# A graph network kernel: runs of edges grouped by destination block and by two source blocks instead of one

## The chip, the cores and the metric

The kernel runs on one core of one Trainium2 chip. The metric is device time in microseconds (us) of one execution. Three runs of the kernel before gave 11165.87, 11168.30 and 11169.82 us; the median is 11168.3.

## The reference

There are 6250 nodes of 32 channels and 106250 directed edges (50000 random pairs in both directions, and one loop per node). Four graph layers follow each other, each as x = x + layer(relu(layernorm(x))): a Gaussian mixture layer, a two-step neighbourhood mean with a hidden width of 64, a spline convolution (with a small network that moves each edge's position) and a two-step neighbourhood sum. Both layers with two steps have this core, used four times in all:

```
summed = segment_sum(x[src], dst, num_segments=N)     # gather rows by source, add them by destination
h = relu(summed/deg @ W_l + b + x @ W_r)
out = segment_sum(h[src] ..., dst) ...                # and again
```

All results are float32.

## The kernel before, in words

Nodes stand in 49 blocks of 128 (NB), node b*128+p in partition p. A "tile" is 128 edge slots, one per partition. Edges are kept in three orders: by source (880 tiles), by destination, and by spline cell. In destination order a tile holds edges of one destination block only.

**Runs.** Within a destination block the edges are also ordered by source block, and each group of one destination block and one source block is padded to a multiple of 8. Eight consecutive slots are a "run" (RUN = 8). `place_by_runs` (lines 686 to 797) works out these places from counts. The worst case of the padding sets the size of everything in destination order: TILES_D = 1008 tiles (line 43), which every loop goes over, filled or not.

**Sending.** `send_runs` (904 to 991) gathers the source rows. Runs are sorted by source block; 128 runs of one source block are a "set", and the table has SSETS = 176 sets (line 48). Per set VectorE compares the eight local numbers of each run with the lane (`hot`, line 940: a one-hot matrix of 128 x 1024), TensorE multiplies each of eight 128 x 128 parts of it with the 112 columns of that source block (line 955, eight slots, each a weight load and a matmul), ScalarE copies the 896 columns out of PSUM into `rec` (line 969), and GpSimd scatters 128 rows of 1792 bytes to `run_rows` in DRAM (line 986). The rings: `loc` (the local numbers, broadcast to all partitions, one 2 MB DMA by SyncE for 8 sets, line 927) has two halves of 8 sets, `hot` and PSUM have 4 places, `rec` has 16. ScalarE refills a half of `rec` when the scatters of that half have landed (line 966). Padding entries have an index beyond the table, so their rows are not written.

**Summing.** `sum_runs` (993 to 1163) reads `run_rows` back in batches of 8 tiles (126 batches) by a plain DMA and adds the rows by destination: per tile a weight load and a matmul of 66 columns and a weight load and a matmul of 33 columns (lines 1075, 1077). The two functions are called four times in turn. In the second call (with `planes`) the same batches also carry the network's outputs of both ends of the edge to GpSimd, which takes their difference.

**Other loops over TILES_D.** `destination_order_pass` (1930 to 2104, 42 turns of 6 batches of 4 tiles) forms the first layer's messages and scatters each tile to the cell order with GpSimd (line 2099). `to_cells` (2325 to 2380) does the like for the spline convolution (line 2375, 63 turns of 16 tiles). The sort by new cell (2554 to 2582) has TILES_D columns and 64 bins. `source_runs` (1177 to 1293) finds each run's place, over DSETS = 126 columns of runs in chunks of 24, and `job_send_ids` scatters their numbers (126 scatters) while the messages are summed. `rec_d` and `run_rows` are blanked by DMAs before use (line 494 and line 422).

The engines keep in step by semaphores written out by hand; stages are divided by barriers (`next_phase`), so a stage's end is that of its last engine.

## Time and profile before

| | |
|---|---|
| median of three runs | 11168.3 us |
| profiled execution | 11236.53 us, span 11234.7 us |
| busy: PE, DVE, ACT, POOL | 54%, 48%, 21%, 61% of the span |
| mean granted TensorE clock | 0.602 of full speed |
| mean DMA rate | 96 GB/s |

PE is TensorE's matmuls and PEld its weight loads, DVE is VectorE, ACT ScalarE, POOL GpSimd, SP SyncE. "L986" is line 986. A row of a group gives the line, engine, operation, what it writes and reads, and the number of times; then the busy time and the mean duration in ns; then the idle time of the engine just before those instructions and what ended it. The lines of the page show a kernel of many stages in which no engine is busy throughout; each stage has to be read by itself. In the granted clock 1.00 is 2.4 GHz and 0.50 is 1.2 GHz.

### The profile page before, as it was taken

To read this page: it belongs to the slowest core of one execution; us is meant where nothing else is said; L and a number is where in the kernel's file an instruction comes from. 1 tells how busy PE (TensorE), PEld (TensorE's weight loads), DVE (VectorE), ACT (ScalarE), POOL (GpSimd) and SP (SyncE) were. 2 spreads that over 40 slices of the span, in tenths; PEclk is the share of its full clock that TensorE was granted. 3 is DMA by queue.
4 is the path that set the end of the run, shared out by engine and by line. 5 is a ranking of instruction groups with operands and counts; after the bars stand their busy time and mean duration, and the time that the engine had idled before them with its cause. 6 is when DMAs were issued, how large, how long until landed. Compare 5 with 4: busy or idle time off the path is not lost. (4 is left out here: it accounts for less than half of the span.)

```text
span 11234.7 us, 164281 instructions
## 1 busy us (share of the span) xinstructions
PE 6072.8 (54%) x41365; PEld 4946.0 (44%) x41366; DVE 5445.1 (48%) x9318; ACT 2323.2 (21%) x6227; POOL 6797.1 (61%) x7082
## 2 busy tenths in 40 slices
PE   5200056665677775666555556655555555554555
PEld 1200035554566674444443445434444444443444
DVE  9300075555555556888783535641111333374535
ACT  0000024443233331111104141011111111124040
POOL 0677727777577776777434146447777777765151
PEclk9555577777555557788656555565555555556565
DMA  9960012221333331111375556762000111126565
GB/s 367 207 63 5 5 44 83 82 83 66 94 100 102 99 100 41 53 53 53 77 157 217 140 208 172 158 54 26 13 13 9 25 28 28 27 51 253 110 248 113
DMA packets 1380904, 1074.85 MB, mean 96 GB/s; under 512 B 949835, under 2 KB 1216095, under 8 KB 1369239
## 3 DMA queue, kind: packets, MB, share of 16 engines
q1 hardware_dynamic: 968054, 604.30, 22.9%
q0 software_dynamic: 239808, 283.02, 8.0%
q10 hardware_dynamic: 172896, 185.88, 5.3%
q8 instruction: 55, 0.90, 0.0%
q14 instruction: 91, 0.75, 0.0%
HBM read 553.90 MB, written 595.42 MB: 102 GB/s over the span
## 5 line engine op out<-in xcount | busy, mean ns | idle before, releaser
L2545 POOL DMA_INDIRECT msg<-msg,idx x1792 | 1744.9, 974 | 587.7 <-issue 530.9
L986 POOL DMA_INDIRECT run_rows<-rec,idx x704 | 730.4, 1038 | 1196.6 <-ACT rec L969 1026.0
L2099 POOL DMA_INDIRECT cell<-rec,idx x1008 | 1070.0, 1062 | 428.7 <-issue 306.0
L2375 POOL DMA_INDIRECT cell<-rec,idx x1008 | 1004.8, 997 | 535.8 <-issue 294.0
L1776 POOL DMA_INDIRECT rec_d<-rec,idx x880 | 909.8, 1034 | 455.6 <-issue 267.0
L404 POOL DMA_INDIRECT rec_r<-sc_rec,sc_idx x832 | 816.6, 982 | 602.2 <-ACT sc_rec L395 316.7
L2525 PE MATMUL ps<-w_stn,hft 128*128 x1792 | 600.6, 494 | 403.0 <-ACT hft L2479 391.8
L2312 PE MATMUL ps<-h_rows,oht 128*128 x2016 | 481.4, 403 | 587.4 <-ACT oht L2319 587.0
L955 PE MATMUL ps<-planes,hot 128*128 x5632 | 495.3, 267 | 533.9 <-ACT rec L969 416.8
L2312 PEld LDWEIGHTS ps<-h_rows,oht 128*128 128x128 f32 x2016 | 448.8, 328 | 687.2 <-issue 687.2
L278 PE MATMUL ps<-mark,column 128*128 128x416 bf16 (+2 forms) x454 | 120.8, 379 | 1106.8 <-DVE mark L209 1100.0
L673 DVE TENSOR_TENSOR oh<-iota_f,rd 128x512 f32<-128x512 f32 x253 | 178.7, 708 | 1096.9 <-PE ps L2297 1096.2
L2525 PE MATMUL ps<-w_conv,hft 128*128 x1792 | 436.2, 424 | 503.8 <-ACT hft L2479 503.8
L955 PEld LDWEIGHTS ps<-planes,hot 128*128 128x128 bf16 x5632 | 421.4, 127 | 608.3 <-issue 584.6
L1092 DVE TENSOR_TENSOR oh<-iota_f,rd 128x1024 bf16<-128x1024 f32 x504 | 597.6, 1228 | 186.9 <-PE ps L1077 185.8
L2017 PE MATMUL ps<-h,oht 128*128 x2016 | 494.1, 427 | 338.1 <-ACT rec L2081 338.1
L1075 PE MATMUL ps<-got,oh 128*128 128x66 bf16 x4032 | 525.6, 233 | 252.9 <-DVE oh L1092 237.2
L2449 DVE TENSOR_REDUCE msg<-wy 128x256 f32<-128x1024 f32 (+1 forms) x448 | 525.8, 1174 | 279.2 <-DMA msg<-msg,idx 262.2
L2525 PEld LDWEIGHTS ps<-w_conv,hft 128*128 128x128 f32 x1792 | 396.0, 325 | 590.4 <-issue 590.3
L2525 PEld LDWEIGHTS ps<-w_stn,hft 128*128 128x128 f32 x1792 | 413.7, 242 | 532.5 <-issue 463.4
L940 DVE TENSOR_SCALAR hot<-loc,lane_c 128x1024 bf16<-128x1024 bf16 x704 | 342.7, 502 | 602.3 <-PE ps L955 542.3
L2017 PEld LDWEIGHTS ps<-h,oht 128*128 128x128 f32 x2016 | 449.2, 328 | 400.9 <-issue 400.9
(422 smaller groups left out, 15118.2 us busy)
## 6 DMA issues: line engine op xcount, KB each, us to landing
loc<-loc_s SPq DMA_DIRECT2D x88, 2048.0 KB
got<-run_rows SPq DMA_DIRECT2D x504, 224.0 KB
got<-rec_d SPq DMA_DIRECT2D x252, 416.0 KB
rec_d<-padd ACTq DMA_DIRECT2D x4, 13312.0 KB
rec_d<-padd ACTq DMA_DIRECT2D x4, 12896.0 KB
cell<-rec,idx POOLq DMA_INDIRECT x2016
loc<-loc_d ACTq DMA_DIRECT2D x126, 256.0 KB
cin<-cell SPq DMA_DIRECT2D x224, 136.0 KB, 2.1
```

Of the source, the lines that this page charges most:

```text
L404: nc.gpsimd.indirect_dma_start(out=table, out_offset=bass.IndirectOffsetOnAxis(ap=s["idx"][:, n, g:g + 1], axis=0), in_=s["rec"][:, n, g, ...
L955: mm = nc.tensor.matmul(ps[:, 2 * (m % RING) + g // HR, g % HR * W:(g % HR + 1) * W], hot[:, m % RING, g * P:(g + 1) * P], flat[:, ds(ids[ ...
L986: nc.gpsimd.indirect_dma_start(out=out, out_offset=bass.IndirectOffsetOnAxis(ap=idx[:, u, m % HU:m % HU + 1], axis=0), in_=rec[:, m, :], i ...
L1092: nc.vector.tensor_tensor(oh[:, n, :, :], bcast(iota_f[:, :].unsqueeze(1), [P, GS, P]), bcast(rd[:, ds(k * GS, GS), LOC].unsqueeze(2), [P, ...
L1776: nc.gpsimd.indirect_dma_start(out=rec_d, out_offset=bass.IndirectOffsetOnAxis(ap=idx[:, n, g:g + 1], axis=0), in_=rec[:, n, g, :], in_off ...
L2017: mm = nc.tensor.matmul(ps[:, 5 + n % 2, g * F:(g + 1) * F], oht[:, n % 2, g, :], nodes[:, ds(ids[g] * F, F)], start=True, stop=True)
L2099: nc.gpsimd.indirect_dma_start(out=cells, out_offset=bass.IndirectOffsetOnAxis(ap=idx[:, n, g:g + 1], axis=0), in_=rec[:, n, g, :], in_off ...
L2312: mm = nc.tensor.matmul(ps[:, 2 + n % 2, g * W:(g + 1) * W], s["oht"][:, n % 2, g, :], nodes[:, ds(ids[g] * pitch, W)], start=True, stop=True)
L2375: nc.gpsimd.indirect_dma_start(out=cells, out_offset=bass.IndirectOffsetOnAxis(ap=idx[:, n, g:g + 1], axis=0), in_=rec[:, n, g, :], in_off ...
L2449: nc.vector.tensor_reduce(msg[:, n, :, 0:F], wy[:, n % 2, :, :, :].rearrange("p g c o -> p g o c"), AX.X, ALU.add).then_inc(s_msg, 1)
L2525: mm = nc.tensor.matmul(ps[:, 2 + banks * (n % 2) + col // 512, col % 512:col % 512 + rest * F], hft[:, n % 2, g, :], w, start=True, stop= ...
L2545: nc.gpsimd.indirect_dma_start(out=msgs, out_offset=bass.IndirectOffsetOnAxis(ap=idx[:, n, g:g + 1], axis=0), in_=msg[:, n, g, :], in_offs ...
```

## The change

A group is now one destination block and one pair of source blocks (SUPER = 2, 256 nodes; NSB = 25 pairs). There are 49 x 25 groups to pad instead of 49 x 49, so the sizes become TILES_D = 944 (118 batches of 8 tiles, 236 of 4, DSETS = 118) and SETS = 136 worked on per sending pass (the table is allocated with SSETS = 144). A source row may lie in either block of its pair, so the one-hot of a set is made twice, for lanes 0 to 127 and 128 to 255, and each of the eight parts is two slots, accumulated in PSUM: 16 slots per set. The block number and the local number of a source are cut at 8 bits instead of 7; the map of source-ordered tiles to blocks is halved in `place_by_runs`; `planes` gets a 50th block of zeros. The loops end on exact counts: with a last turn of 8 sets in `send_runs`, of 4 batches in `sum_runs`, and of 2 batches in `destination_order_pass`.

```diff
...
+SUPER = 2
+NSB = -(-NB // SUPER)
...
-TILES_D = -(-((E + (RUN - 1) * NB * NB + NB * (P - RUN)) // P + 1) // STEP) * STEP
+TILES_D = -(-((E + (RUN - 1) * NB * NSB + NB * (P - RUN)) // P + 1) // STEP) * STEP
 UBD = 6
-NTD = -(-((E + (RUN - 1) * NB * NB + NB * (P - RUN)) // P + 1) // (UBD * G))
-assert NTD * UBD * G <= TILES_D
+KD_ALL = TILES_D // G
+NTD = -(-KD_ALL // UBD)
 DSETS = TILES_D * QUADS // P
-SSETS = -(-(((E + (RUN - 1) * NB * NB) // RUN + NB * (P - 1)) // P + 1) // 16) * 16
+SETS = -(-(((E + (RUN - 1) * NB * NSB) // RUN + NSB * (P - 1)) // P) // 8) * 8
+SSETS = -(-SETS // 16) * 16
...
-                    then(nc.vector.tensor_copy(lane_c[:, :], lane_i[:, :]))
+                    for u in range(SUPER):
+                        then(nc.vector.tensor_scalar(lane_c[:, u:u + 1], lane_i[:, :], float(u * P), None, ALU.add))
...
+                        then(nc.vector.tensor_scalar(tb_i[:, :], tb_i[:, :], SUPER.bit_length() - 1, None, ALU.arith_shift_right))
...
+                        then(nc.vector.tensor_scalar(map_i[:, :], map_i[:, :], SUPER.bit_length() - 1, None, ALU.arith_shift_right))
...
-                        sort_map(then, w2, "s", NB)
+                        sort_map(then, w2, "s", NSB)
...
+                            then(nc.vector.memset(planes[:, NB:, :], 0.0))
+                            split_planes(then, planes[:, 0:NB, :], h_nm[:, :, :], rest[:, :, :])
...
-            TURNS = SSETS // UNROLL
-            assert TURNS * UNROLL == SSETS
+            FULL, TAIL = SETS // UNROLL, SETS % UNROLL
+            assert TAIL in (0, HU)
             flat = planes[:, :, :].rearrange("p b w -> p (b w)")
             out = run_rows.rearrange("(u i) w -> u (i w)", i=RUN)
             with ExitStack() as c:
-                loc, hot = sb_in(c, "loc", [P, 2, HU, RUN * P], BF16), sb_in(c, "hot", [P, RING, RUN * P], BF16)
+                loc, hot = sb_in(c, "loc", [P, 2, HU, RUN * P], BF16), sb_in(c, "hot", [P, RING, SUPER, RUN * P], BF16)
...
+                def all_sets(eng, turn):
+
+                    with eng.Fori(0, FULL) as i:
+                        turn(i, UNROLL)
+                    if TAIL:
+                        turn(FULL, TAIL)
...
-                                nc.vector.tensor_scalar(hot[:, m % RING, :], loc[:, u, m % HU, :], lane_c[:, 0:1], None,
-                                                        ALU.is_equal).then_inc(s_hot, 1)
+                                for w in range(SUPER):
+                                    made = nc.vector.tensor_scalar(hot[:, m % RING, w, :], loc[:, u, m % HU, :], lane_c[:, w:w + 1], None,
+                                                                   ALU.is_equal)
+                                made.then_inc(s_hot, 1)
...
-                                    ids = block_ids(ENG.PE, "s", i * UNROLL + m, NB - 1, HU)
+                                    ids = block_ids(ENG.PE, "s", i * UNROLL + m, NSB - 1, HU)
                                 pe.wait_ge(s_hot, k + 1 + UNROLL)
                                 pe.wait_ge(s_fill, k + 1)
                                 for g in range(RUN):
-                                    mm = nc.tensor.matmul(ps[:, 2 * (m % RING) + g // HR, g % HR * W:(g % HR + 1) * W], hot[:, m % RING, g * P:(g + 1) * P],
-                                                          flat[:, ds(ids[m % HU] * W, W)], start=True, stop=True)
+                                    for w in range(SUPER):
+                                        mm = nc.tensor.matmul(ps[:, 2 * (m % RING) + g // HR, g % HR * W:(g % HR + 1) * W],
+                                                              hot[:, m % RING, w, g * P:(g + 1) * P],
+                                                              flat[:, ds(ids[m % HU] * (SUPER * W) + w * W, W)],
+                                                              start=(w == 0), stop=(w == SUPER - 1))
...
-            TURNS = TILES_D // (GS * RING)
+            K = TILES_D // GS
+            FULL, TAIL = K // RING, K % RING
...
-                        then(nc.vector.memset(empty[:, :, :].rearrange("p b w -> p (b w)").bitcast(BF16), 255.0))
+                        then(nc.vector.memset(empty[:, :, :].rearrange("p b w -> p (b w)").bitcast(BF16), float(P * SUPER)))
...
-                        then(nc.vector.tensor_scalar(block_i[:, :], runs_i[:, :, 0], 7, None, ALU.arith_shift_right))
+                        then(nc.vector.tensor_scalar(block_i[:, :], runs_i[:, :, 0], (P * SUPER).bit_length() - 1, None, ALU.arith_shift_right))
...
+                def counted(i):
+
+                    return min(UBD, KD_ALL - i * UBD)
+
+                def exists(i, n):
+
+                    return not isinstance(i, int) or i * UBD + n < KD_ALL
...
-                        with pool.Fori(0, NTD) as i:
-                            for n in range(UBD):
...
+                        with pool.Fori(0, NTD - 1) as i:
+                            turn(i, UBD)
+                        turn(NTD - 1, counted(NTD - 1))
                         for n in range(UBD):
-                            pool.wait_ge(sent[n], 16 * G * NTD)
+                            pool.wait_ge(sent[n], 16 * G * (NTD - 1 + (1 if n < counted(NTD - 1) else 0)))
...
```

## Rows read from the trace of the kernel before

**Rows 1.** The page: engine totals; costliest groups (busy us, mean ns | idle before, releaser)
```profile
PE 6072.8 (54%) x41365; PEld 4946.0 (44%) x41366; DVE 5445.1 (48%) x9318; ACT 2323.2 (21%) x6227; POOL 6797.1 (61%) x7082
...
L986 POOL DMA_INDIRECT run_rows<-rec,idx x704 | 730.4, 1038 | 1196.6 <-ACT rec L969 1026.0
L2099 POOL DMA_INDIRECT cell<-rec,idx x1008 | 1070.0, 1062 | 428.7 <-issue 306.0
L2375 POOL DMA_INDIRECT cell<-rec,idx x1008 | 1004.8, 997 | 535.8 <-issue 294.0
...
L940 DVE TENSOR_SCALAR hot<-loc,lane_c 128x1024 bf16<-128x1024 bf16 x704 | 342.7, 502 | 602.3 <-PE ps L955 542.3
```

**Rows 2.** L986 alone in each sending pass (duration min/median/max, first and last start)
```profile
L986 POOL DMA_INDIRECT run_rows<-rec,idx x176: 967/975/1312, 6001.4 to 6247.0; - x176
...
L986 POOL DMA_INDIRECT run_rows<-rec,idx x176: 967/974/1310, 6572.2 to 6820.9; - x176
...
L986 POOL DMA_INDIRECT run_rows<-rec,idx x176: 967/975/1311, 10186.8 to 10428.1; - x176
...
L986 POOL DMA_INDIRECT run_rows<-rec,idx x176: 967/975/1310, 10751.1 to 10990.3; - x176
```

**Rows 3.** Windows of the first sending pass
```profile
core 0: us, PE busy (x) PEld busy (x) DVE busy (x) ACT busy (x) POOL busy (x), PEclk, DMA share, GB/s
6001.00:6201.00 200.00, 97.99 (x1153) 82.08 (x1150) 70.53 (x145) 117.60 (x161) 146.08 (x141) 0.70 0.86 315
6201.00:6251.00 50.00, 19.26 (x224) 15.76 (x224) 12.19 (x24) 26.41 (x35) 36.35 (x36) 0.64 0.25 93
```

**Rows 4.** Waits in the first sending pass: total us, times, longest us
```profile
ACT idx L967 <- DMA run_rows<-rec,idx: 90.4, 17, 11.5
...
PE ps L955 <- DVE hot L940: 12.2, 6, 9.0
```

**Rows 5.** Timeline of the first sending pass: start us, us, instruction, idle before it
```profile
6002.77 3.05 DVE L940 TENSOR_SCALAR hot<-loc,lane_c 128x1024 bf16<-128x1024 bf16 x7 [1.22 <-PE ps L955]
...
6004.08 1.27 POOL L986 DMA_INDIRECT run_rows<-rec,idx  x1 [0.30 <-ACT rec L969]
```

**Rows 6.** Windows of line 955 alone: two bursts of 32 slots without a gap
```profile
core 0: us, PE busy (x) PEld busy (x), PEclk, DMA share, GB/s
6048.66:6051.77 3.11, 3.10 (x32) 2.76 (x32) 0.50 0.18 71
6071.98:6073.57 1.59, 1.58 (x32) 1.59 (x32) 1.00 0.89 346
```

**Rows 7.** First and last start of the scatters of L2099 and of L2375
```profile
L2099 POOL DMA_INDIRECT cell<-rec,idx x1008: 971/972/1760, 2907.2 to 4283.2; - x168
...
L2375 POOL DMA_INDIRECT cell<-rec,idx x1008: 970/972/1502, 7423.8 to 8737.4; - x168
```

**Rows 8.** SyncE's loads of a summing pass: without, then with, the edge differences
```profile
6255.60 207.24 SPq L1034 DMA_DIRECT2D got<-run_rows  x126
...
6829.43 352.23 SPq L1034 DMA_DIRECT2D got<-run_rows  x126
```

**Rows 9.** The last sort (window), and its merge beside one of 880 columns
```profile
7205.00:7404.00 199.00, 106.20 (x386) 28.73 (x386) 179.75 (x241) 0.00 (x0) 0.00 (x0) 0.86 0.48 84
...
L232 DVE COPY_PREDICATED rank<-mark,ps 128x1008 f32<-128x1008 int16 x64 | 81.4, 1272 | 1.8 <-PE ps L293 1.6
...
L232 DVE COPY_PREDICATED rank<-mark,ps 128x880 f32<-128x880 int16 x49 | 55.5, 1132 | 1.6 <-PE ps L293 1.5
```

**Rows 10.** The page's group of the run shifts
```profile
L1240 PE MATMUL ps<-delta,quads 64*128 64x64 f32 x252 | 54.2, 418 | 5.7 <-ACT quads L1250 4.3 <-DVE sel L1285 1.4
```

**Rows 11.** Blanking beside the first sort, and the message summing over its stretch
```profile
15.90 262.51 ACTq L494 DMA_DIRECT2D rec_d<-padd  x8
...
299.88 0.35 SPq L310 DMA_DIRECT2D map_c<-tbi  x1
...
5563.00:5860.00 297.00, 168.12 (x2644) 146.28 (x2642) 282.26 (x657) 0.00 (x0) 146.92 (x121) 0.54 0.83 191
```

More of the change, by code:

```diff
@@ L923, in _, with turn @@
                     def _(sp):
-                        with sp.Fori(0, TURNS) as i:
-                            for u in range(2):
+                        def turn(i, count):
+                            for u in range(count // HU):
                                 sp.wait_ge(s_hot, i * UNROLL + (u + 1) * HU)
@@ L929, in _, with turn @@
                                                    [P, HU * RUN * P])).then_inc(s_ld[u], 16)
+                        all_sets(sp, turn)
                     @block.vector
                     def _(v):
-                        nc.vector.sem_inc(s_hot, UNROLL)
-                        with v.Fori(0, TURNS) as i:
-                            for m in range(UNROLL):
+                        def turn(i, count):
+                            for m in range(count):
                                 k, u = i * UNROLL + m, m // HU
@@ L976, in _, with turn @@
                         last_row = nc.gpsimd.to_reg(DSETS * P - 1)
-                        with pool.Fori(0, TURNS) as i:
-                            for m in range(UNROLL):
+                        def turn(i, count):
+                            for m in range(count):
                                 u = m // HU
@@ L1027, in _, with turn @@
                     def _(sp):
-                        with sp.Fori(0, TURNS) as i:
-                            for n in range(RING):
+                        def turn(i, count):
+                            for n in range(count):
                                 k = i * RING + n
@@ L1043, in _, with turn @@
                                            planes[:, b0:b0 + nb, 3 * AW:3 * AW + 12]).then_inc(s_table, 1)
-                        with act.Fori(0, TURNS) as i:
-                            for n in range(RING):
+                        def turn(i, count):
+                            for n in range(count):
                                 k = i * RING + n
@@ L1143, in _, with turn @@
                         nc.gpsimd.sem_inc(s_new, 1)
-                        with pool.Fori(0, TURNS) as i:
-                            for n in range(RING):
+                        def turn(i, count):
+                            for n in range(count):
                                 k = i * RING + n
@@ L1951, in _, with turn @@
                         load_weights(sp, s_w)
-                        with sp.Fori(0, NTD) as i:
-                            for n in range(UBD):
+                        def turn(i, count):
+                            for n in range(count):
                                 k = i * UBD + n
@@ L1975, in message, with turn @@
                                                     AX.X, ALU.add).then_inc(s_m0, 1)
-                        def turn(i, last):
-                            for n in range(UBD):
+                        def turn(i, count):
+                            for n in range(count):
                                 k = i * UBD + n
-                                if not last or n + AHEAD < UBD:
+                                if exists(i, n + AHEAD):
                                     prepare(i + (n + AHEAD) // UBD, k + AHEAD, (n + AHEAD) % UBD)
@@ L2006, in turn_hot, with turn @@
                             tr.then_inc(s_turned, 1)
-                        def turn(i, first, last):
-                            for n in range(UBD):
+                        def turn(i, count, first):
+                            for n in range(count):
                                 k, t = i * UBD + n, i * (UBD * G) + n * G
-                                if not (last and n == UBD - 1):
+                                if exists(i, n + 1):
                                     turn_hot(k + 1, n + 1)
@@ L2058, in copy_turned, with turn @@
                                            turned[n % 2]).then_inc(s_copied, 1)
-                        def turn(i, first, last):
-                            for n in range(UBD):
+                        def turn(i, count, first):
+                            for n in range(count):
                                 k, t = i * UBD + n, i * (UBD * G) + n * G
-                                if not last or n < UBD - 2:
+                                if exists(i, n + 2):
                                     cast(k + 2, n + 2)
@@ L2093, in _, with turn @@
                         last_row = nc.gpsimd.to_reg(P * TC - 1)
-                        with pool.Fori(0, NTD) as i:
-                            for n in range(UBD):
+                        def turn(i, count):
+                            for n in range(count):
                                 pool.wait_ge(s_fill, i * UBD + n + 1 + UBD)
```

128 lines of the change are left out of this document (75 added, 53 removed).

## The prediction

> **What bounds the kernel now.** I read the page first: no engine is busy throughout, GpSimd most with 61%, and of its time the scatters named in [rows 1] run once per tile or set, whatever is in it. So I looked at each stage that the change shortens, for what sets its pace. In the sending pass the reader is to compare the first start and the last start of the 176 scatters [rows 2]: 245.6, 248.7, 241.3 and 239.2 us, mean 243.7. The windows of the first pass [rows 3] show two regimes. For 200 us the DMA engines are 86% busy at 315 GB/s and GpSimd starts 141 scatters; in the last 50 us the DMA rate falls to 93 GB/s, and GpSimd goes on at its own pace, one scatter per 0.974 us plus 0.30 us to the next = 1.274 us. The wait of ScalarE for scatters to land, 90.4 us in 17 waits [rows 4], says the same: in the first regime transfers hold the ring back. TensorE waits for VectorE only 12.2 us there. In the destination pass and in the cell pass GpSimd is the bound: from first to last start 1376.0 us and 1313.6 us for 1007 steps [rows 7], so 1.366 and 1.304 us per tile, near the same 1.274, with idle times that are mostly "issue" [rows 1]. A summing pass takes 207.2 us for 126 batches, 1.645 us each, and the one with the edge differences 352.2 us, 2.795 us each [rows 8].
>
> **The counts.** The sizes follow from the diff: 176 to 136 sets, 1008 to 944 tiles. Counted over the reference's edges, the groups give 14309 real runs before and 13812 after, real sets 146 and 122, and real tiles 917 and 881. So of the 40 sets that go, 24 were real ones and 16 padding; of the 64 tiles, 36 and 28.
>
> **Sending, the part that could go either way.** Bytes: a set loads 128 x 2048 B = 0.262 MB of local numbers, a real run scatters 1792 B. Before, up to the last real set: 146 x 0.262 + 14309 x 0.001792 = 63.9 MB, at the 315 GB/s of [rows 3] 203 us; the remaining 30 sets at 1.3 us give 39, together 242, against 243.7 measured. The model fits, so I use it. After: 122 x 0.262 + 13812 x 0.001792 = 56.7 MB, 180 us, and 14 empty sets x 1.274 = 18: 198 us. The other engines must be able to follow:
> - GpSimd: 136 x 1.274 = 173 us, and a surcharge. A scatter beside a comparison takes 1.27 us where it is 0.975 at the median [rows 2, 5]; the mean is 1.038, so 0.063 us x 176 = 11 us per pass with 176 comparisons. The change makes 272 of them: 17 us. Floor 190 us, under 198.
> - VectorE: 272 x 0.502 us [rows 1] = 137 us.
> - TensorE: 32 slots took 3.11 us at a granted clock of 0.50 and 1.59 us at 1.00 [rows 6], so 97 or 50 ns each. A set has 16 slots: 1.56 or 0.80 us; a pass 212 or 109 us. At the lower level (1.2 GHz) this is above 198, at the upper (2.4 GHz) far below. Before, with 0.78 or 0.40 us per set, neither level mattered. The mean clock was 0.70 with TensorE half busy [rows 3].
> I take 202 us: the transfer model, with 4 us for stretches at the lower clock. Bounds for the unknown mix: 190 (GpSimd's floor, if fewer bytes leave the queues free) and 228 (TensorE at 1.2 GHz, 212, with 16 us of waits). Saved: 243.7 - 202 = 42 us per pass, four times 167 us.
>
> The Trainium skill bears on two points here. GPSIMD Engine Reference, 1. Specifications: GpSimd's SBUF interfaces are shared with VectorE, and instructions in a two-port mode contend. It speaks against the change, which doubles such comparisons; the 1.27 us row agrees in direction, and the measured surcharge is used. TensorE: Matmul & The Clock Gate, Part 1: activity releases the throttle and an idle stretch brings it back. By it, denser matmuls hold the upper level more of the time and TensorE would need 109 us, so that only the transfer bound is left.
>
> **Destination pass and cell pass.** Every tile costs GpSimd the same scatter, real or not. Destination: 36 real tiles x 1.37 and 28 empty x 1.28, which is 85 us; I take 86 (all 64 at the mean pace: 87). Cell pass: 64 x 1.304 = 83 us. Bounds: 82 (all at 1.274 us) to 87 each. What is late next is nothing new: TensorE's and ScalarE's work per tile falls in the same number. The destination pass now ends with short turns written out after the loop; that this costs is bounded by one pipeline filling, a few us, inside the range.
>
> **Summing.** 8 batches fewer per pass: 3 x 8 x 1.645 = 39.5 us and 8 x 2.795 = 22.4 us. TensorE's 32 instructions per batch are the same; the bound doesn't move. 62 us.
>
> **The last sort.** 64 columns fewer in 64 bins. The merge fell from 1272 to 1132 ns over 128 columns [rows 9], so 70 ns x 64 = 4.5 us; all 199 us in proportion would be 12.6. I take 8: VectorE is busy 180 of the 199 us and all its wide operations shrink, but with a fixed part each.
>
> **Source runs.** 126 columns cost TensorE 54.2 us [rows 10], 0.43 us each; 8 fewer: 3.4 us.
>
> **What costs or is hidden.** Blanking `rec_d` is 6% shorter but ends at 278 us, beside a sort whose map is stored at 300 [rows 11]: nothing. Blanking `run_rows` and the 8 fewer number scatters lie beside the message summing, where VectorE is busy 282 of 297 us [rows 11]: nothing, at most 8 x 1.27 = 10 us if they were the end. Added on VectorE, in chains: two shifts before the ranks, one on 64 x 880 numbers, and a 112-column memset twice: the nearest row of many columns is [rows 9]'s 1.1 us, so under 2 us. No wait is added; existing waits guard the same rings, and SyncE's load of a half still follows the half's last comparison, now after two comparisons per set; at 8 x 1.0 us against a half's 8 x 1.4 us it has room. I count +2 us.
>
> **Sum.** 167 + 86 + 83 + 62 + 8 + 3.4 - 2 = 407 us. The rows come from an execution of 11236.5 us (span 11234.7); the three runs have a median of 11168.3, a factor of 0.9939. 11236.5 - 407 = 10829.5; times 0.9939 gives 10763. Forecast 10760 us, faster by 3.7%.
>
> **Rivals.**
> - *TensorE at 1.2 GHz becomes the bound of the sending passes.* For it: 16 slots at 97 ns are 1.56 us, more than the 1.46 us per set that 198 us leave, and the sample at 0.50 is from the pass itself; its bursts break off when ScalarE waits for landings [rows 4], after which the clock must be won again. Against: a fully busy TensorE is what came before the rise in such a pass, and `rec` is 16 sets deep. Pass 212 plus about 10 = 222 us; saved 22 x 4 = 87 instead of 167; total 327, time (11236.5 - 327) x 0.9939 = 10843. Chance 0.22.
> - *The transfers get out of the way and GpSimd's issue is the bound,* 190 us per pass: 54 x 4 = 215, total 455, time 10716. For it: fuller sets, fewer bytes between two landings. Against: bytes per real set grow from 0.438 to 0.465 MB. Chance 0.12.
> - *The tiles don't pay.* If another engine set the pace of the destination and cell passes behind GpSimd's short gaps, half of the 169 us would stay: total 323, time 10847. Against: idle before the scatters is "issue" in most of both [rows 1]. Chance 0.04.
> - *The passes serialise, and the kernel gets slower.* If comparison pair, 16 slots and copy no longer overlap, because a ring of four is too short for the longer steps at 1.2 GHz, a set costs 1.0 + 1.56 + 0.8 = 3.4 us (the last from 117.6 us of ScalarE over some 143 sets in [rows 3]), a pass 460 us. That is 216 x 4 = 865 lost against 240 won elsewhere: time 11789. It decides from 243.7 + 60 = 304 us per pass, 2.2 us per set. Against: TensorE waits for VectorE only 12.2 us [rows 4] with the same ring. Chance 0.02.
>
> **How the numbers follow.** The forecast has 0.60, its own range 10735 to 10795 (198 to 210 us per pass, the bounds of the other terms). The range for 8 in 10 takes in the second rival's middle and the first's upper bound of 228 us: 10700 to 10865. Faster by over 0.2% (about what a measurement of this kernel can tell from no change): all cases but the last, and a little for what no row shows: 0.97; within 0.2%: 0.01; slower: 0.02.
>
> **What would show it.** Right: four passes of 195 to 210 us between the first and the last scatter of line 986 (136 each); 944 scatters in the destination and cell passes at 1.37 and 1.30 us; 118 loads per summing pass at 1.65 and 2.80 us; DMA rate near 315 GB/s until the real sets end. The first rival shows as ScalarE waiting for TensorE in the passes at a granted clock near 0.5 and over 215 us; the second as 1.40 us per set with no waits for landings. The forecast is wrong if a pass is above 228 or below 190 us, or if a stage with fewer tiles keeps its length.

## The result and the profile after

The changed kernel takes 10747.0 us (median of 4 runs, 10742.9 to 10762.4); the kernel before, run beside it, 11168.5 us. The ratio is 0.9625, 95% interval 0.9612 to 0.9639: 421 us saved, where 407 of the profiled execution, some 405 after scaling, were forecast. The time forecast was 10760 us.

The page of the changed kernel, in the form of [rows 1]: engine totals, then the groups of the scatters, of the matmuls and of the comparisons of the sending pass.

```profile
PE 5932.8 (55%) x43331; PEld 4877.0 (45%) x43332; DVE 5442.2 (51%) x9592; ACT 2152.9 (20%) x5870; POOL 6471.3 (60%) x6754
...
L1017 POOL DMA_INDIRECT run_rows<-rec,idx x544 | 599.1, 1101 | 1120.5 <-ACT rec L995 992.5
L2448 POOL DMA_INDIRECT cell<-rec,idx x944 | 932.3, 988 | 504.4 <-issue 279.3
L2168 POOL DMA_INDIRECT cell<-rec,idx x944 | 975.0, 1033 | 407.8 <-issue 286.3
...
L975 PE MATMUL ps<-planes,hot 128*128 x8704 | 535.8, 230 | 313.7 <-ACT rec L995 193.3
...
L957 DVE TENSOR_SCALAR hot<-loc,lane_c 128x1024 bf16<-128x1024 bf16 x1088 | 462.1, 492 | 292.5 <-PE ps L975 240.9
```

704 scatters have become 544, and their mean has risen from 1038 to 1101 ns. The first and second sending passes and the two passes over tiles answer to [rows 2] and [rows 7] (duration min/median/max, first and last start):

```profile
L1017 POOL DMA_INDIRECT run_rows<-rec,idx x136: 967/1032/1312, 5877.7 to 6072.2; - x136
...
L1017 POOL DMA_INDIRECT run_rows<-rec,idx x136: 967/980/1306, 6384.5 to 6577.5; - x136
...
L2168 POOL DMA_INDIRECT cell<-rec,idx x944: 971/972/1729, 2883.4 to 4144.6; - x189
...
L2448 POOL DMA_INDIRECT cell<-rec,idx x944: 969/972/1491, 7144.9 to 8363.5; - x189
```

The four passes take 194.5, 193.0, 194.3 and 195.3 us, mean 194.3. A tile costs 1261.2 / 943 = 1.337 us in the destination pass and 1218.6 / 943 = 1.292 us in the cell pass. The windows and the waits of the first pass answer to [rows 3] and [rows 4]:

```profile
5880.00:6030.00 150.00, 104.97 (x1770) 100.12 (x1767) 93.57 (x224) 90.91 (x121) 117.82 (x106) 0.89 0.91 338
```

```profile
ACT idx L993 <- DMA run_rows<-rec,idx: 65.5, 15, 7.6
DVE hot L957 <- PE ps L975: 62.2, 43, 5.9
PE ps L975 <- ACT rec L995: 51.9, 23, 6.0
...
PE ps L975 <- DVE hot L957: 13.0, 4, 10.6
```

TensorE is 70% busy and is granted 0.89 of full speed, where it was half busy at 0.70. VectorE waits for TensorE (62.2 us) far more than TensorE for VectorE (13.0 us), as it did before, where 542.3 us of VectorE's idle time over the four passes were ended by TensorE [rows 1]. GpSimd's own time adds up to nearly the whole pass: 136 scatters of 1.101 us and 135 gaps of 0.30 us are 190.2 us, so beyond the gaps it idles about 4 us. The summing passes answer to [rows 8]:

```profile
6077.41 197.69 SPq L1074 DMA_DIRECT2D got<-run_rows  x118
6582.75 330.03 SPq L1074 DMA_DIRECT2D got<-run_rows  x118
```

197.7 / 118 = 1.675 and 330.0 / 118 = 2.797 us per batch; the other two took 195.2 and 194.9 us.

### The profile page after: what moved, and what is told of

Its sections match the earlier page's. It is cut to its first block and busy times, and to the rows that moved or that the text cites. A ratio compares the mean times of both kernels' runs of the same rounds, so it can differ in the third digit from the quotient of the medians.

```text
span 10741.1 us, 165184 instructions
## 1 busy us (share of the span) xinstructions
PE 5932.8 (55%) x43331; PEld 4877.0 (45%) x43332; DVE 5442.2 (51%) x9592; ACT 2152.9 (20%) x5870; POOL 6471.3 (60%) x6754
## 5 line engine op out<-in xcount | busy, mean ns | idle before, releaser
L1017 POOL DMA_INDIRECT run_rows<-rec,idx x544 | 599.1, 1101 | 1120.5 <-ACT rec L995 992.5
L2448 POOL DMA_INDIRECT cell<-rec,idx x944 | 932.3, 988 | 504.4 <-issue 279.3
L2168 POOL DMA_INDIRECT cell<-rec,idx x944 | 975.0, 1033 | 407.8 <-issue 286.3
L2385 PE MATMUL ps<-h_rows,oht 128*128 x1888 | 450.9, 403 | 537.4 <-ACT oht L2392 537.0
L975 PE MATMUL ps<-planes,hot 128*128 x8704 | 535.8, 230 | 313.7 <-ACT rec L995 193.3
L975 PEld LDWEIGHTS ps<-planes,hot 128*128 128x128 bf16 x8704 | 511.6, 108 | 338.6 <-issue 333.8
L1139 DVE TENSOR_TENSOR oh<-iota_f,rd 128x1024 bf16<-128x1024 f32 x472 | 560.1, 1230 | 179.3 <-PE ps L1116 178.4
L1114 PE MATMUL ps<-got,oh 128*128 128x66 bf16 x3776 | 492.8, 233 | 238.5 <-DVE oh L1139 223.7
L2085 PE MATMUL ps<-h,oht 128*128 x1888 | 462.7, 427 | 289.1 <-ACT rec L2147 289.1
L957 DVE TENSOR_SCALAR hot<-loc,lane_c 128x1024 bf16<-128x1024 bf16 x1088 | 462.1, 492 | 292.5 <-PE ps L975 240.9
L1860 PE MATMUL ps<-xgs,oht 128*128 x2640 | 400.0, 296 | 355.0 <-ACT rec L1775 354.7
```

What stands on the lines that cost most here:

```text
L975: mm = nc.tensor.matmul(ps[:, 2 * (m % RING) + g // HR, g % HR * W:(g % HR + 1) * W], hot[:, m % RING, w, g * P:(g + 1) * P], flat[:, ds(i ...
L1017: nc.gpsimd.indirect_dma_start(out=out, out_offset=bass.IndirectOffsetOnAxis(ap=idx[:, u, m % HU:m % HU + 1], axis=0), in_=rec[:, m, :], i ...
L1114: nc.tensor.matmul(sums[:, ds(at[of + g], PAIR)], oh[:, n, g, :], part[n][:, g, 0:PAIR], start=False, stop=False)
L1139: nc.vector.tensor_tensor(oh[:, n, :, :], bcast(iota_f[:, :].unsqueeze(1), [P, GS, P]), bcast(rd[:, ds(k * GS, GS), LOC].unsqueeze(2), [P, ...
L2168: nc.gpsimd.indirect_dma_start(out=cells, out_offset=bass.IndirectOffsetOnAxis(ap=idx[:, n, g:g + 1], axis=0), in_=rec[:, n, g, :], in_off ...
L2385: mm = nc.tensor.matmul(ps[:, 2 + n % 2, g * W:(g + 1) * W], s["oht"][:, n % 2, g, :], nodes[:, ds(ids[g] * pitch, W)], start=True, stop=True)
```

## The experiments

**Both kernels again.** The profiled execution of the kernel before was 68 us above the median of its runs. A second profile of each shows where.

> The kernel before, unchanged, for a second profile. Its profiled execution was 68 us above the median of its own runs, while that of the changed kernel was at its median. Theory A (the excess of 68 us belonged to that one execution and lay in stages with scatters or large transfers, which the change doesn't touch by itself): the new profile spans 11165 to 11180 us, the sending passes take 235 to 240 us instead of 244, and the destination pass (first to last scatter) some 1360 us instead of 1376. Rival B (profiling itself slows the kernel before by 0.6%): the new profile again spans 11225 to 11240 us with the same stages. Ratio to the kernel before 1.000 in both.

> The changed kernel, unchanged, as a control on this chip: ratio 0.9625 within 0.002, four sending passes of 193 to 196 us from first to last scatter.

Measured 11173.3 us (ratio to before 1.0004, interval 0.9993 to 1.0015) and 10745.4 us (0.9615, 0.9598 to 0.9632). The kernel before now takes 240.4, 239.3, 238.3 and 239.4 us for its sending passes (mean 239.4) and 1341.7 us from the first to the last scatter of the destination pass, so the excess belonged to the first profile, as theory A says, and was larger in the destination pass than it said. The passes of the changed kernel are 193.9, 198.0, 191.8 and 196.6 us (mean 195.1); two of them lie outside the 193 to 196 expected. The profiled executions have spans of 11166.3 and 10751.6 us, so they can be compared stage by stage without a factor. A stage here runs from one first start on SyncE to the next (us):

| stage | before, 1st profile | before, 2nd | after, 2nd | saved, 2nd to 2nd | forecast |
|---|---|---|---|---|---|
| first sort, `rec_d` blanked | 314.6 | 315.0 | 304.5 | 10.5 | 0 |
| destination pass | 1424.7 | 1390.8 | 1315.5 | 75.3 | 86 |
| source runs | 70.2 | 70.3 | 74.7 | -4.4 | 3.4 |
| four sending passes | 1056.7 | 1038.2 | 858.1 | 180.0 | 167 |
| three summing passes | 678.8 | 678.3 | 640.7 | 37.5 | 39.5 |
| summing with edges, last sort | 571.8 | 572.4 | 539.8 | 32.6 | 30.4 |
| cell pass | 1328.6 | 1321.9 | 1241.6 | 80.3 | 83 |

The 68 us of the first profile are its own: 34 lie in the destination pass and 18.5 in the sending passes, and are gone in the second. What made them is open. The source order between the first sort and the destination pass, which the change leaves alone, took 1283 and 1281 us. The table's savings are 412 us, of 414.7 between the two spans.

**The pair of blocks undone, in two ways.** The change does two things: it pairs source blocks, and it takes smaller sizes that the pairs permit. In the first of these kernels the sizes follow from single blocks; in the second they are set by hand to 944 tiles and 152 sets, which these edges fit into (917 real tiles, 146 real sets).

```diff
-SUPER = 2
+SUPER = 1
...
-SETS = -(-(((E + (RUN - 1) * NB * NSB) // RUN + NSB * (P - 1)) // P) // 8) * 8
+SETS = 152
...
```

The last two lines and `TILES_D = 944` are in the second kernel alone.

> The changed kernel with SUPER = 1: groups of one destination and one source block again (1008 tiles, one comparison and 8 slots per set), but with the loops ending on exact counts, which makes 168 sets per pass instead of 176. Theory (an empty set costs GpSimd's pace of 1.274 us): 4 x 8 x 1.274 = 41 us less than the kernel before, 11127 us, ratio 0.9963. Rival (the short last turns, written out after the loops, cost something of their own, 5 us or more per place): 11140 us or more.

> As the last one, SUPER = 1, but with the table sizes set by hand to 944 tiles and 152 sets, which hold this input's 917 real tiles and 146 real sets. So the tile loops are those of the change, while a pass still has 146 real sets of 8 slots. Theory (real sets cost transfers, 0.438 MB each at 315 GB/s, with TensorE and VectorE hidden in both): passes of 203 + 6 x 1.27 = 211 us, against 194 in the changed kernel, so 10747 + 4 x 17 = 10815 us. Rival 1 (TensorE's or VectorE's doubled work costs the changed kernel real time): a pass here comes out at 200 us or less, 10770 or less. Rival 2 (the tile loops gain from fuller tiles, not from fewer): the destination pass stays above 1290 us instead of 1261.

Measured 11120.3 us (0.9952, 0.9935 to 0.9969) and 10789.9 us (0.9662, 0.9642 to 0.9681). Against the medians of the same group, 11173.2 us for the kernel before and 10745.4 for the changed one, the count of tiles as before saves 53 us, 944 tiles and 152 sets save 383, and the whole change 428. All of it but 44 us is therefore had without the pairs, on these edges. What the pairs do is to make 944 tiles enough for any 106250 edges on these nodes. The first kernel saves 37 us in its sending stages, where 41 were expected in all, so the last turns written out behind the loops cost nothing that shows; the other 16 us are spread over stages that it leaves as they were. In the second, the scatters of the destination pass span 1254.8 us, so fewer tiles and not fuller ones make it shorter, and its sending passes, at 207 us, are longer than the changed kernel's 194, so neither of its rivals holds. Most of the 44 us follows from the scatters too; here is the first pass with 152 sets of one comparison and eight slots, and the page's row of its scatters:

```profile
L1018 POOL DMA_INDIRECT run_rows<-rec,idx x152: 967/973/1312, 5869.1 to 6076.1; - x152
...
L1018 POOL DMA_INDIRECT run_rows<-rec,idx x608 | 625.7, 1029 | 1140.1 <-ACT rec L996 995.2
```

Its passes average 207.3 us. The changed kernel has 16 sets fewer, which at 1.029 + 0.30 us are 21.3 us, and gives back 136 x (1.101 - 1.029) = 9.8 us: 11.5 us a pass by this sum, where the passes differ by 13.0 (first profile of the changed kernel) or 12.2 (second).

**What sets a sending pass.** Three kernels change one load each. The first makes one comparison per set and lets all 16 slots read it; the second makes both comparisons and one matmul per slot; the third adds a load that nothing reads.

```diff
-                                for w in range(SUPER):
+                                for w in range(1):
                                     made = nc.vector.tensor_scalar(hot[:, m % RING, w, :], loc[:, u, m % HU, :], lane_c[:, w:w + 1], None,
...
-                                                              hot[:, m % RING, w, g * P:(g + 1) * P],
+                                                              hot[:, m % RING, 0, g * P:(g + 1) * P],
```

> The changed kernel with the second comparison of each set left out: both slots of a part use the one-hot of lanes 0 to 127 (so rows of odd source blocks are not picked and the output is not the reference's). 16 slots, bytes and scatters stay. In the changed kernel GpSimd is idle only 4 us in a pass beyond its gaps of 0.30 us: 136 x 1.101 + 135 x 0.30 = 190 of 194 us, and a scatter takes 1.101 us on average against 0.974 alone. Theory G (GpSimd's own pace, with the surcharge of the comparisons, now bounds the pass): the mean scatter falls to 1.03 to 1.04 us and a pass to 184 to 187 us, 10745 - 4 x 8.5 = 10711 us. Rival D (the transfers bound it, as forecast): the scatters get shorter but the pass stays at 193 to 196 us, 10745 us.

Measured 10712.4 us (0.9594, 0.9578 to 0.9610), passes of 185.6, 191.5, 189.2 and 189.6 us, mean 189.0. Its page has

```profile
L1017 POOL DMA_INDIRECT run_rows<-rec,idx x544 | 563.6, 1036 | 1137.7 <-ACT rec L995 1003.0
```

The mean scatter is back at the 1038 ns of [rows 1]: the second comparison costs 65 ns per scatter, against the 63 of the prediction, or 8.8 us a pass, and the pass is 5.3 us shorter. GpSimd's time and the pass move together, the rest going into waits. The median is what theory G gave, the pass lies between its 184 to 187 and the rival's 193 to 196: this supports that GpSimd sets most of the pace, with transfers close behind.

```diff
                                 for g in range(RUN):
-                                    for w in range(SUPER):
+                                    for w in range(1):
...
-                                                              start=(w == 0), stop=(w == SUPER - 1))
+                                                              start=True, stop=True)
...
```

> The changed kernel with one slot per part, 8 instead of 16 per set, of lanes 0 to 127 only (the same rows are not picked, the output is not the reference's); both comparisons are made. Theory G and rival D: TensorE is hidden, a pass stays at 191 to 196 us, 10735 to 10750 us, and the granted clock in the pass falls from 0.9 to about 0.7. Rival P (TensorE's doubled work is what holds the pass above the 190 us of GpSimd): 188 us or less, 10720 or less.

Measured 10770.3 us (0.9641, 0.9623 to 0.9658): with half of its matmuls it is no faster than the changed kernel, and 58 us slower than the kernel with one comparison, which ran beside it. The passes were 203.1, 203.5, 208.4 and 200.4 us, mean 203.9, which neither theory expected; the granted clock fell to 0.67 as expected. The profile is of the slowest of the four runs, 26 us above the median. TensorE is not what the changed kernel waits for, so the first rival of the prediction falls; and something that TensorE held back comes forward. In what follows, a train is a number of comparisons on VectorE with no gap of 0.15 us or more between them; a timeline shows it as one row, with their number behind the x. Two timelines of this kernel's first pass, VectorE then GpSimd (start us, us, instruction, idle before it), show it:

```profile
5879.63 12.76 DVE L957 TENSOR_SCALAR hot<-loc,lane_c 128x1024 bf16<-128x1024 bf16 x32 [9.05 <-DMA loc<-loc_s]
5893.31 6.42 DVE L957 TENSOR_SCALAR hot<-loc,lane_c 128x1024 bf16<-128x1024 bf16 x16 [0.92 <-PE ps L975]
```

```profile
5884.28 8.96 POOL L1017 DMA_INDIRECT run_rows<-rec,idx  x1 [261.09 <-ACT rec L995]
5893.54 1.17 POOL L1017 DMA_INDIRECT run_rows<-rec,idx  x1 [0.30 <-ACT rec L995]
5895.02 4.84 POOL L1017 DMA_INDIRECT run_rows<-rec,idx  x1 [0.30 <-ACT rec L995]
5900.15 0.97 POOL L1017 DMA_INDIRECT run_rows<-rec,idx  x1 [0.30 <-issue]
```

The scatter that takes 8.96 us instead of 0.97 starts within a train of 32 comparisons, and ends 0.85 us after the train; the one of 4.84 us ends at 5899.86, 0.13 us after the train that ended at 5899.73. This kernel has 11 scatters over 1.5 us, which are 44.8 us above 0.975 us each in all, or 11 us per pass, and its passes are 14.9 us longer than those with one comparison.

```diff
...
+                                sp.wait_ge(s_more, 16 * (2 * i + u + 1))
+                                sp.dma_start(more[:, :],
+                                             bcast(loc_s[ds((i * UNROLL + u * HU) * RUN * P, HU * RUN * P // 2)].unsqueeze(0),
+                                                   [P, HU * RUN * P // 2])).then_inc(s_more, 16)
...
```

> The changed kernel with 1 MB more loaded for every 8 sets, into a tile that nobody reads, beside the 2 MB of local numbers: 60.5 + 17.8 = 78.3 MB per pass, 72.7 of them before the last real set. Rival D: at 315 to 340 GB/s a pass takes 214 to 231 us plus 18 for the empty sets, 232 to 249 us, 10745 + 4 x 46 = 10930 us. Theory G in its strong form (transfers have room to spare): under 205 us, 10790 or less. In between, both are near each other and take turns.

Measured 10814.3 us (0.9682, 0.9666 to 0.9698), passes of 213.8, 214.9, 210.5 and 209.6 us. The window of its first pass:

```profile
5880.00:6030.00 150.00, 95.82 (x1502) 91.60 (x1500) 82.53 (x194) 79.63 (x107) 103.49 (x95) 0.85 1.00 400
```

17.8 MB more per pass cost 18 us. The mean pass, 212.2 us, is above the 205 of the strong form of theory G and below the 232 and more of the transfer theory. GpSimd's own time is 136 x 1.092 + 135 x 0.30 = 189.0 us of 212.2 here, so now the transfers do hold it back. The queues moved 400 GB/s with all their time used. The 315 GB/s of [rows 3], at a share of 0.86, was thus no ceiling; as the kernel with more loads moves a larger part of its bytes by the 2 MB and 1 MB loads, its 400 need not be the ceiling of the other kernels' mix.

**Comparisons, matmuls and loads, crossed.** These four ran on a chip that took 12633.0 us for the kernel before, 13% longer, so only runs of this group are compared with each other, and the times in their expectations, which come from the faster chips, can't be met. The changed kernel itself was not run in this group. The stages of the scatter chains are longer there (source order 1543 us instead of 1284), the summing passes are not (212 us); the cause is open.

```diff
-                                sp.dma_start(loc[:, u, :, :].rearrange("p b e -> p (b e)"),
+                                sp.dma_start(loc[:, u, 0:HU // 2, :].rearrange("p b e -> p (b e)"),
...
+                            nc.vector.memset(loc[:, u, HU // 2:, :], -1.0).then_inc(s_clear, 1)
```

This is the edit of the two kernels with half the loads; the other edits are those shown above.

> The same program as c2_one_slot (one selection matmul per slot instead of two, so the second block of each pair is not picked), run again. Two readings of its 10770 us and of its first pass of 203.1 us with scatters of up to 8.96 us. N, an accident of single executions, as were the 68 us of the first profile of the kernel before: no scatter above 5 us in this profile, passes of 191 to 196 us, median near 10740. L, a lasting effect of half the matmuls: passes of 200 to 208 us again, a granted clock of 0.67 over 5880:6030 and a median of 10760 to 10780.

> One comparison and one matmul per slot, as in the kernel before, but with the 136 sets of the changed one (left out: the second block of each pair). If GpSimd with the comparisons' surcharge sets the pass (G), and the matmuls matter only through it, 185 to 192 us as with one comparison alone (185.5 to 191.5), 10712. If half the matmuls cost by themselves (L), each pass is again some 8 to 12 us longer than with one comparison alone: 195 to 203 us, median 10745 to 10760.

> Only the first 4 of every 8 sets' local numbers are loaded; the other places hold -1 from one memset ahead of each pass, so those sets pick nothing, while every comparison, matmul, copy and scatter still runs. The pass moves 42.7 MB instead of 60.5. Read from first to last scatter, since the memset lies before. G (GpSimd's issue with the surcharge sets the pace): 190 to 193 us per pass, at most 4 us less than the changed kernel's 194.5. D (transfers set it, at 315 to 340 GB/s, up to the last real set): bytes no longer bind, so the pass falls to GpSimd's floor too; but then scatters of under 1.10 us mean or gaps under 0.30 us would have to show, and with an uncongested queue below 188 us. ScalarE's waits for landings, 88 us in the first pass of the changed kernel, fall in both. Median 10745 to 10765 with the memsets of some 10 us per pass added.

> Half the loads as in d3_half_loads and one matmul per slot as in c2_one_slot (left out: half the sets' picks and the second block of each pair). If the longer passes of c2_one_slot come from transfers that run late (loads and scatters meeting), they are gone: 190 to 193 us. If they come from TensorE or its clock, they stay, 8 to 12 us above d3_half_loads: 198 to 205 us.

| kernel | comparisons, matmuls per slot, loads | median us, ratio to before (interval) | passes us | scatters over 1.5 us, their excess |
|---|---|---|---|---|
| d1 | 2, 1, all | 12177.9, 0.964 (0.9624 to 0.9657) | 246.2, 240.1, 228.5, 230.7 | 31, 150.6 us |
| d2 | 1, 1, all | 12094.1, 0.9575 (0.9559 to 0.9591) | 219.9, 214.7, 216.2, 214.5 | 0 |
| d3 | 2, 2, half | 12200.3, 0.9657 (0.9641 to 0.9673) | 241.7, 239.0, 227.1, 234.8 | 8, 51.3 us |
| d4 | 2, 1, half | 12282.6, 0.9726 (0.9710 to 0.9743) | 250.2, 260.4, 248.6, 260.6 | 22, 215.3 us |

The means of the passes are 236.4, 216.3, 235.7 and 255.0 us. The kernel with half the matmuls has its long scatters again, and with one comparison per set it has none and its passes are 20.1 us shorter, 84 us of the median. So they were no accident of one execution, and they are no cost of having few matmuls by themselves: they need the second comparison. Halving the loads doesn't cure it: with one matmul per slot the passes become 18.6 us longer by it, and with half the loads the kernel with half the matmuls is 19.3 us a pass above the one with both. The excess of the scatters, 37.7 us a pass in d1, is more than the 20.1 us, so part of it falls into time in which the pass would have waited anyway. VectorE and GpSimd in the first pass with half the loads and one matmul per slot:

```profile
6780.20 19.10 DVE L958 TENSOR_SCALAR hot<-loc,lane_c 128x1024 bf16<-128x1024 bf16 x48 [6.23 <-DMA loc<-loc_s]
```

```profile
6784.89 15.25 POOL L1021 DMA_INDIRECT run_rows<-rec,idx  x1 [419.67 <-ACT rec L999]
6800.45 0.97 POOL L1021 DMA_INDIRECT run_rows<-rec,idx  x1 [0.30 <-issue]
```

What remains is this: a pair of comparisons per set makes VectorE run in long trains as soon as TensorE and the loads let it, and a scatter can be shut out for the rest of a train. In the eight profiles of kernels with two comparisons per set (the changed one has 2 and 4 in its two, those with more loads and with the split store below 1 each) there are 80 scatters over 1.5 us. Each ran beside a train of 8 to 48. 55 of them ended 0.12 to 0.13 us behind the train's end, 14 ended 0.84 to 0.87 us behind it, 12 of these being the first of a pass, and 11 ended 0.8 to 3.2 us before it. Kernels with one comparison per set have trains of at most 8 and nearly no such scatter: 0 in three of them and in both profiles of the kernel before, and one of 1.67 us with single blocks and 168 sets. The Trainium skill has the mechanism: SBUF — State Buffer, SBUF: two separate sides, calls the port pair of VectorE and GpSimd an exclusive lock, and says under A bandwidth-pool intuition that's wrong that a GpSimd DMA is blocked until some 115 ns after VectorE's instruction has ended; the 0.12 to 0.13 us here agree, but behind a train of up to 42 instructions, not behind one. That it is this lock is a reading of these times; no run here keeps the comparisons off that port. Not every train does it. In the changed kernel's first pass four scatters pass beside one of 16 comparisons at the small surcharge, 1.22 to 1.28 us each; three of them:

```profile
5889.39 6.42 DVE L957 TENSOR_SCALAR hot<-loc,lane_c 128x1024 bf16<-128x1024 bf16 x16 [2.42 <-DMA loc<-loc_s]
```

```profile
5890.70 1.28 POOL L1017 DMA_INDIRECT run_rows<-rec,idx  x1 [0.30 <-issue]
5892.28 1.28 POOL L1017 DMA_INDIRECT run_rows<-rec,idx  x1 [0.30 <-issue]
5893.86 1.28 POOL L1017 DMA_INDIRECT run_rows<-rec,idx  x1 [0.30 <-issue]
```

What decides between 0.3 us and a whole train is open. So is what filled the passes with half the loads: they should have come down to GpSimd's time, 136 x 1.136 + 135 x 0.30 = 195 us with both matmuls, and took 235.7, with transfers at 47% of the queues' time in the first. The halved loads are not the cause: with all loads and one comparison the same sum, 136 x 0.991 + 135 x 0.30 = 175 us, falls short of 216.3 by the same 41 us, where on the faster chips it falls short by 4 to 9 (23 with more loads). On this chip something else than GpSimd's own time sets the pass, so that run doesn't separate the two theories it was made for.

**The store that got slower.** Source runs took 4.4 us more with 8 columns fewer. SyncE's timeline, before (second profile) and after:

```profile
5450.31 0.35 SPq L1206 DMA_DIRECT2D src_d<-h  x1
5453.97 0.40 SPq L1208 DMA_DIRECT2D runs<-src_d  x1
```

```profile
5355.02 0.27 SPq L1260 DMA_DIRECT2D src_d<-h  x1
5367.83 0.40 SPq L1262 DMA_DIRECT2D runs<-src_d  x1
```

The load that waits for the store starts 3.66 us after it where 126 partitions were stored, and 12.81 us after it where it is 118. The windows between the two, before and after (in the last two columns the busy share of the 16 DMA engines and GB/s):

```profile
5450.70:5453.70 3.00, 1.80 (x9) 1.83 (x9) 0.71 (x1) 3.00 (x2) 0.00 (x0) 0.52 0.63 172
```

```profile
5355.50:5367.50 12.00, 10.89 (x51) 10.92 (x52) 0.63 (x1) 4.01 (x3) 0.00 (x0) 0.54 0.14 42
```

A share of 0.14 over 12 us is the time of 2.2 engines. Both stores of 118 partitions were then split; the first:

```diff
-                        sp.dma_start(src_d.rearrange("(q p l) -> p q l", q=8, l=P), by_tile[0:QT, :, :]).then_inc(s_io, 16)
-                        sp.wait_ge(s_io, 16)
+                        to = src_d.rearrange("(q p l) -> p q l", q=8, l=P)
+                        for p0, p1 in ((0, 112), (112, QT)):
+                            sp.dma_start(to[p0:p1], by_tile[p0:p1, :, :]).then_inc(s_io, 16)
+                        sp.wait_ge(s_io, 32)
...
```

> The changed kernel with the two stores of source_runs from 118 partitions cut into 112 and 6 partitions. In the changed kernel 12.8 us pass from the issue of the store of src_d to the load behind it, in the kernel before (126 partitions) 3.7 us, and the stage takes 74.7 instead of 70.3 us though it has 8 columns fewer. Theory (a store from 118 partitions runs on few DMA engines): 4 to 5 us between the two, the stage 66 us, 9 us less in all: 10736 us; by the time alone this is at the edge of what can be told, the stage decides. Rival (the store is slow for another reason, as what it writes to or what runs beside it): 12 us again. The Trainium skill, page DMA: Bandwidth & Descriptors, section on why a DMA increments its semaphore by 16, says that a transfer is spread over the largest number of engines up to 16 that divides its outer dimension, which would be 2 for 118 and 14 for 126.

```profile
5358.82 0.85 SPq L1262 DMA_DIRECT2D src_d<-h  x2
5362.30 0.39 SPq L1264 DMA_DIRECT2D runs<-src_d  x1
```

Now it is 3.48 us, and the stage takes 65.7 us instead of 74.7. The kernel takes 10728.9 us (10724.2 to 10731.2; ratio 0.9608, 0.9592 to 0.9625) and is the fastest of those that leave nothing out: its slowest run is 8 us below the changed kernel's fastest in either group, though the intervals overlap. Of the 18 us between the medians 9 are the stage's; 6 more lie between the chips, as the kernel before took 11162.3 us beside this one and 11168.5 beside the changed one. The Trainium skill, DMA: Bandwidth & Descriptors, Why a DMA increments its semaphore by 16 and not by 1, says that a transfer is spread over the largest number up to 16 that divides its outer size: 14 for 126 partitions, 2 for 118, 16 for 112. The three gaps agree, and so do the shares.

## Why the prediction was right, step by step

- **Destination and cell pass, 86 and 83 us.** Right in mechanism and nearly in size: 75 and 80. A tile costs one scatter, real or not. The pace of the second profile, 1341.7 / 1007 = 1.332 us, would have given the same 85 for the destination pass; what is missing is that the tiles that stay cost a little more than that, 1.337 and 1.341 us in the two profiles of the changed kernel, which over 943 steps are 5 to 8 us. Why is open.
- **Sending passes, 167 us.** 180 measured, 45 per pass instead of 42. The number is near, but the bound that was named is not the one that the runs show, and that the two agree is in part luck. The prediction had transfers "at the 315 GB/s of [rows 3]" hold GpSimd back, before and after, with 198 us for the new pass. In that very window of 200 us GpSimd is busy 146.1 us, and 141 gaps of 0.30 us make it 188. Over a whole pass of the kernel before (second profile) its own time is 176 x 1.032 + 175 x 0.30 = 234.2 of 239.4 us; in the changed kernel it is 190.2 of 194.3. So the fall of GpSimd's own time, 44 us, is nearly all of the 45. ScalarE's waits for landings, 90.4 us then and 65.5 now, were read as GpSimd's; the 16 places of `rec` cover nearly all of them. The bytes were right, but 315 GB/s was no ceiling: the queues move 338 in the changed kernel and 400 with more to do, and only there do they hold GpSimd back by much (23 us a pass). The pass lies just under the 195 to 210 us that the prediction gave as a sign of being right. The mechanism is that of the second rival (chance 0.12), whose floor of 190 us was worked out rightly, with 4 us of waits on top of it.
- **The surcharge on the scatters.** Forecast as 0.063 us per comparison, 17 us a pass; measured (1.101 - 0.975) x 136 = 17.1 us. Taken as an average it hid a second form, the scatter shut out for a train, which cost the changed kernel 5 to 10 us in all and could have cost it 45.
- **TensorE at 1.2 GHz, chance 0.22.** Didn't come: the granted clock rose with TensorE's load, 0.70 to 0.89, and half the matmuls made no pass shorter.
- **Summing 62 us, last sort 8.** 37.5 and 32.6 = 70.1, as forecast (69.9).
- **"Blanking `rec_d` ... nothing."** Wrong: 10.5 us. The 262.51 us of [rows 11] run from the first to the last issue, and the last eighth takes 35 us more: in the second profile of the kernel before the last packet of ScalarE's queue ends at 313.7 us. Two windows of that profile, then two of the changed kernel (the last two columns are the DMA share and GB/s):

```profile
305.00:310.00 5.00, 0.00 (x0) 0.00 (x0) 0.00 (x0) 0.00 (x0) 0.00 (x0) 0.50 1.03 402
310.00:315.00 5.00, 0.00 (x0) 0.00 (x0) 0.00 (x0) 0.00 (x0) 0.00 (x0) 0.50 0.67 266
```

```profile
290.00:295.00 5.00, 2.40 (x12) 0.77 (x10) 4.79 (x7) 0.00 (x0) 0.00 (x0) 1.00 0.89 347
295.00:300.00 5.00, 0.00 (x0) 0.00 (x0) 4.78 (x7) 0.00 (x0) 0.00 (x0) 0.80 0.01 2
```

  SyncE's timeline of the kernel before (second profile) and of the changed one, whose blanking is 6% shorter; the second line of each starts the next stage:

```profile
306.38 0.21 SPq L313 DMA_DIRECT2D maps_c<-map_c  x1
315.03 0.33 SPq L592 DMA_DIRECT2D g_sb<-in_L_gnn_g  x1
```

```profile
302.72 0.21 SPq L316 DMA_DIRECT2D maps_c<-map_c  x1
305.17 0.33 SPq L596 DMA_DIRECT2D g_sb<-in_L_gnn_g  x1
```

  From the small load to the next stage it took 8.65 us, then 2.45. The kernels with 1008 tiles end this stage at 314.6 to 315.9 us, those with 944 at 303.8 to 305.2, with or without pairs. In the three profiles with 1008 tiles (the kernel before twice, single blocks once) the stage ends 1.4 us behind the blanking's last packet, at 313.2 to 314.5 us. With 944 tiles that packet comes at 294.6 to 301.2 us, ahead of the sort's own last load, and the stage ends with the sort. So some 10 us is what the blanking stuck out in the kernel before.
- **Source runs, 3.4 us.** Wrong in sign: the columns' gain was eaten by one store over 118 partitions.
- **The factor 0.9939.** It spread 68 us evenly that lay mainly in two stages; since it scaled the saving by only 2.5 us, no harm came of it.

The misses, +10.5 (first sort), -7.8 (source runs) and +13 (sending) against -11 and -3 (passes over tiles), leave under 3 us. The total is nearer than its terms, and that is luck: nothing ties these misses to each other.

## What to carry to other kernels

Where one scatter per tile sets the pace, count the instructions, padding included; a change of layout that tightens the proven bound pays for each place that goes, and trying the smaller size by hand shows what the layout itself adds. When an average surcharge appears on GpSimd beside VectorE, look at the longest instruction as well as the mean: work that is sped up elsewhere can join VectorE's instructions into trains. After each change of a size look at the outer dimension of every transfer that it touches, and at the landing, not the issue, of the last transfer that is said to be hidden.

## What the runs showed of the hardware

- A scatter from GpSimd takes 0.97 us alone and 1.27 to 1.28 beside a wide bf16 comparison, and up to 15.3 us when it is shut out by a train of them on VectorE.
- The DMA queues moved 400 GB/s at a busy share of 1.00, in a mix of broadcast loads and scattered rows of 1792 B, and 402 GB/s while a table was blanked.
- A store over 118 partitions delays what waits for it by 12.8 us from its issue, over 126 by 3.7, in two parts of 112 and 6 by 3.5.
- One chip ran the kernel before in 12633 us, the others in 11162 to 11173. The ratio of the one changed program that ran on both kinds, with one matmul per slot, was 0.9640 there and 0.9641 here, though its stages were not longer in the same proportion.
